# Mixture layers computed by expert: rows sorted through DRAM instead of every token through every expert

## The reference

```python
x = x + 0.5 * _L0_ffn_ref(_layernorm(x, axis=-1), L0_ffn_router_w, ...)
x = x + _L0_attn_ref(_layernorm(x, axis=-1), L0_attn_Wq, ...)
x = x + 0.5 * _L0_ffn_ref(_layernorm(x, axis=-1), L0_ffn_router_w, ...)
```

```python
h_norm = layer_norm(h, rn_g, rn_b)
g = jax.nn.softmax(jnp.einsum('bsd,ed->bse', h_norm, router_w), axis=-1)
top2_w, top2_idx = jax.lax.top_k(g, 2)
top2_w = top2_w / (jnp.sum(top2_w, axis=-1, keepdims=True) + EPS_GATE)
hid = jnp.einsum('bsd,edh->bseh', h, w1)
hid = jax.nn.relu(layer_norm(hid, ln_g, ln_b))
expert_out = jnp.einsum('bseh,ehd->bsed', hid, w2)
...
out = jnp.sum(top2_out * top2_w[..., None], axis=-2)
return layer_norm(out, on_g, on_b)
```

## Time and profile before

| | us |
|---|---|
| median of 3 runs (1240.02 to 1240.84) | 1240.5 |
| span of the profiled execution | 1236.4 |
| PE / DVE / POOL / ACT busy in it | 1140.2 / 948.3 / 672.0 / 512.8 |
| one block of a mixture layer (8 a layer) | 52.2 |
| one block of attention (8) | 35 |

### The profile page before, as it was taken

The page is one execution under the profiler, slowest core; times in us unless marked ns, Lnnn a source line. Parts: engine busy times, 40 slices in busy tenths (PEclk is TensorE's granted clock), DMA queues, the critical chain, the costliest instruction groups (busy, mean ns, idle before and its releaser), DMA issues.

```text
span 1236.4 us, 25066 instructions
## 1 busy us (share of the span) xinstructions
PE 1140.2 (92%) x8694; PEld 731.9 (59%) x8694; DVE 948.3 (77%) x2150; ACT 512.8 (41%) x878; POOL 672.0 (54%) x1039
## 2 busy tenths in 40 slices
PE   4669799999999999889999999889999999999996
PEld 4335456656566566656666666556566665666664
DVE  5678787887978878657777777578879787797875
ACT  4353324233342424456665666442333424334131
POOL 2365546454565544498778777543555654546360
PEclk9789989999999999999999999899999999999998
DMA  9002000000000000000000000000000000000000
GB/s 286 4 1 69 1 1 2 1 2 1 0 0 0 1 2 1 19 18 15 11 13 18 17 18 18 1 2 2 17 1 18 1 19 18 0 17 1 19 18 17
DMA packets 29037, 20.69 MB, mean 17 GB/s; under 512 B 7812, under 2 KB 27784, under 8 KB 28808
## 3 DMA queue, kind: packets, MB, share of 16 engines
q1 hardware_dynamic: 24112, 18.36, 5.4%
q10 hardware_dynamic: 4824, 1.07, 0.5%
HBM read 11.03 MB, written 4.19 MB: 12 GB/s over the span
## 4 chain that ended last, share of the span: by engine, by line
PE 48%; DVE 19%; issue 16%; POOL 10%; ACT 4%; DMA 2%; DVEq 1%; ACTq 0%; POOLq 0%
PE bank L1547 7%; PE bank L1549 6%; PE bank L1548 6%; DVE area L674 5%; DVE area L682 4%; PE bank L1532 4%; PE bank L1534 4%; PE bank L1533 4%; DVE area L655 4%; PE bank L1506 4%; POOL area L487 3%; PE bank L1555 2%; PE bank L1557 2%; PE bank L1556 2%; DMA betas<-in_L_ffn_ln_b_dram 2%
## 5 line engine op out<-in xcount | busy, mean ns | idle before, releaser
L1256 ACT ACTIVATE area<-area 128x512 f16<-128x512 f32 x256 | 160.9, 630 | 387.9 <-DVE area L674 386.1
L1547 PE MATMUL bank<-w2h,area 128*128 128x256 f16 x1024 | 281.3, 275 | 12.9 <-DVE area L693 7.2
L1548 PE MATMUL bank<-w2l,area 128*128 128x256 f16 x1024 | 280.5, 274 | 0.0
L1549 PE MATMUL bank<-w2h,area 128*128 128x256 f16 x1024 | 280.5, 274 | 0.0
L674 DVE SCALAR_TENSOR_TENSOR area<-area,betas,bank 128x512 f32<-128x512 f32 x256 | 189.9, 743 | 46.0 <-PE bank L1534 37.6
L682 DVE SCALAR_TENSOR_TENSOR area<-area 128x512 f16<-128x512 f32 x256 | 188.7, 737 | 20.3 <-ACT area L1256 17.1
L1532 PE MATMUL bank<-hTh,w1h 128*128 128x512 f16 x512 | 195.5, 382 | 6.7 <-DVE area L674 6.7
L1533 PE MATMUL bank<-hTl,w1h 128*128 128x512 f16 x512 | 195.1, 381 | 0.0
L1534 PE MATMUL bank<-hTh,w1l 128*128 128x512 f16 x512 | 194.9, 381 | 0.0
L696 DVE SCALAR_TENSOR_TENSOR area<-bank,coef,area 128x256 f32<-128x256 f32 x192 | 92.1, 482 | 79.3 <-PE bank L1549 78.1
L487 POOL TENSOR_TENSOR area<-area 128x512 f16<-128x512 f32 x96 | 119.9, 1274 | 45.1 <-ACT area L1300 44.9
(11 more groups left out here) (233 smaller groups left out, 2109.6 us busy)
## 6 DMA issues: line engine op xcount, KB each, us to landing
X<-in_L_attn_x_dram SPq DMA_DIRECT2D x8, 512.0 KB, 7.1
area<-area SPq DMA_DIRECT2D x128, 32.0 KB, 2.0
out_dram<-X SPq DMA_DIRECT2D x7, 512.0 KB, 2.9
area<-in_L_ffn_w_dram SPq DMA_DIRECT2D x4, 512.0 KB, 9.9
X<-in_L_ffn_w_dram SPq DMA_DIRECT2D x2, 1024.0 KB, 15.7
area<-in_L_ffn_ln_g_dram ACTq DMA_DIRECT2D x1, 1024.0 KB, 6.1
out_dram<-X SPq DMA_DIRECT2D x4, 128.0 KB, 1.7
area<-in_L_attn_Wq_dram SPq DMA_DIRECT2D x1, 256.0 KB, 9.2
```

The lines of the kernel that those rows point to most:

```text
L1256: act.activation(Rh[:, e % 2, m, :], V[:, a % NV], ACT.Relu).then_inc(s_Rh, 1)
L1547: pe.matmul(dst, Rh[:, e % 2, k, rows], w2h[:, e, k, :], start=(k == 0), stop=False)
L1548: pe.matmul(dst, Rh[:, e % 2, k, rows], w2l[:, e, k, :], start=False, stop=False)
L1549: last = pe.matmul(dst, Rl[:, e % 2, k, rows], w2h[:, e, k, :], start=False, stop=(k == HC - 1))
```

## The change

The loops are written out, and a mixture layer becomes two groups of 16 tiles (GT = 16). For a group, the tokens' normed rows (high and low half, 1 KB a row) are made first, with the router's logits and the two best experts of each token. From counts over all 16 tiles (prefix, 17 small matmuls) DVE works out each row's place in a list that is sorted by expert, each expert's part rounded up to whole tiles of 128 rows: 35 slot tiles (NJ = 2 x 16 + 3). POOL scatters the rows to this list in DRAM (scatter, 32 indirect DMAs of 128 rows, one for each tile and choice). SP loads slot tiles back four ahead (load_slots). PE reads the slot tile's expert number from a table into a register (expert) and takes the expert's weights by this register: transposes, Gram, layer 1 (24 matmuls of 128 columns), layer 2 of the slot before (12 of 256). ACT scales the result (scale_out), SP stores it to DRAM (store_slots), and after the group's 35 slots POOL gathers two rows for each token (gather, two indirect DMAs a tile); ACT and DVE weigh, add and norm them and add to X (first_weighted, token_sum, token_out; add_offset on POOL adds the norm's offset to X ahead). Both lists are cleared first (4.6 MB each, by a transfer of SP), since ends are read too.

Group 1's rows, router and scatter stand inside group 0's slots, group 0's gathers inside group 1's slots from slot 38 on (C_AT). Group 0's rows and scatter stand ahead of slot 0, group 1's gathers behind slot 69. Attention starts when the last tile is added (c_x at NT), mixture 2's rows follow attention's last update. ln_b is loaded as one contiguous row. The cores of the diff:

```diff
+            def load_slots(S):
+                G, J = group(S)
+                if J == 0:
+                    sp.wait_ge(sc_h[G % 2], 16 * 2 * GT * (G // 2 + 1))
+                if S < R_HS:
+                    sp.wait_ge(zeroed[0], 16)
+                wait(sp, b_T, S - R_HS + 1)
+                wait(sp, b_h2, S - R_HS + 1)
+                sp.dma_start(hs[:, S % R_HS].rearrange("p c d -> p (c d)"),
+                             slots_in[G % 2][J * P:(J + 1) * P, :]).then_inc(l_hs[S % R_HS], 16)
+            def store_slots(S):
+                G, J = group(S)
+                sp.wait_ge(b_Y, S + 1)
+                if J == 0 and G >= 2:
+                    sp.wait_ge(c_acc, GT * (G - 1))
+                sp.dma_start(slots_out[G % 2][J * P:(J + 1) * P, :], ysb[:, S % R_Y]).then_inc(st_y[S % R_Y], 16)
+            def mixture(f):
+                S0, S1 = f * SF, (f + 1) * SF
+                for S in range(S0, S0 + 4):
+                    load_slots(S)
+                for S in range(S0, S1 + 2):
+                    if S - 2 >= S0:
+                        store_slots(S - 2)
+                    if S + 4 < S1:
+                        load_slots(S + 4)
 
...
+            def scatter(G):
+                pool.wait_ge(r_pos, G + 1)
+                pool.wait_ge(r_hl, GT * (G + 1))
+                if G < 2:
+                    pool.wait_ge(zeroed[G], 16)
+                else:
+                    pool.wait_ge(b_h2, NJ * (G - 1))
+                for t in range(GT):
+                    for k in range(2):
+                        pool.indirect_dma_start(slots_in[G % 2],
+                                                bass.IndirectOffsetOnAxis(pos[:, G % 2, k, t:t + 1], 0),
+                                                hrow[:, t].rearrange("p c d -> p (c d)"), None
+                                                ).then_inc(sc_h[G % 2], 16)
...
+            def slot_std(S):
+                pool.wait_ge(b_ve, S + 1)
+                wait(pool, b_Y, S - 3)
+                k = S % 4
+                pool.tensor_tensor(stds[:, k], vare[:, k:k + 1].to_broadcast([P, 2]), expo[:, :],
+                                   ALU.pow).then_inc(b_sd, 1)
...
+            def gather(i):
+                G, t = i // GT, i % GT
+                if t == 0:
+                    for r in range(R_Y):
+                        pool.wait_ge(st_y[r], 16 * uses(NJ * (G + 1), r, R_Y))
+                wait(pool, c_acc, i - R_C + 1)
+                for k, d in enumerate((yA, yB)):
+                    pool.indirect_dma_start(d[:, i % R_C], None, slots_out[G % 2],
+                                            bass.IndirectOffsetOnAxis(pos[:, G % 2, k, t:t + 1], 0)
+                                            ).then_inc(g_y[i % R_C], 16)
...
+            def mixture(f):
+                G = 2 * f
+                for k in range(GQ):
+                    quad_rstd(GQ * G + k)
+                    quad_again(GQ * G + k)
+                if f == 0:
+                    for e in range(E):
+                        w1_low(e)
+                scatter(G)
+                if f == 0:
+                    pool.wait_ge(p_mx, 2)
+                    pool.partition_all_reduce(mxa2[:, :], mx2[:, :], P, RMAX).then_inc(p_mxa, 1)
+                    for e in range(E):
+                        w2_low(e)
+                for t in range(GT):
+                    add_offset(GT * G + t)
+                S0 = f * SF
+                slot_std(S0)
+                slot_std(S0 + 1)
+                for s in range(SF):
+                    t = s + 2 - A_AT
+                    if 0 <= t < GT and t % TB == 0:
+                        quad_rstd(GQ * (G + 1) + t // TB)
+                    if s + 2 < SF:
+                        slot_std(S0 + s + 2)
+                    t = s + 1 - A_AT
...
+                    if s == CHAIN_AT + 1:
+                        scatter(G + 1)
+                    t = s - C_AT - 2
+                    if 0 <= t < GT:
+                        token_rstd(GT * G + t)
+                    t = s - C_AT
+                    if 0 <= t < GT:
+                        gather(GT * G + t)
+                for t in range(GT + 1):
+                    if t < GT:
+                        gather(GT * (G + 1) + t)
+                    if t >= 1:
+                        token_rstd(GT * (G + 1) + t - 1)
...
+            def expert(S):
+                G, J = group(S)
+                if J == 0:
+                    pe.wait_ge(r_tab, G + 1)
+                return pe.value_load(etab[0:1, G % 2, J:J + 1], min_val=0, max_val=E - 1)
...
+            def layer1(S, e):
+                pe.wait_ge(b_sdr, S + 1)
+                wait(pe, b_Rl, S - 1)
+                if S == 0:
+                    pe.wait_ge(p_w1l, E)
+                a = hT[:, S % R_HT]
+                for m in range(HC):
+                    o = bank[S % 2][:, m * P:(m + 1) * P]
+                    cols = slice(m * P, (m + 1) * P)
+                    for c in range(KC):
+                        pe.matmul(o, w1h[:, bass.ds(e, 1), c, cols], a[:, c], start=(c == 0), stop=False)
+                        pe.matmul(o, w1h[:, bass.ds(e, 1), c, cols], a[:, KC + c], start=False, stop=False)
+                        last = pe.matmul(o, w1l[:, bass.ds(e, 1), c, cols], a[:, c], start=False, stop=(c == KC - 1))
...
+                for S in range(S0, S1):
+                    s = S - S0
+                    if S + 3 < S1:
+                        slots_T(S + 3)
+                    t = s - A_AT
+                    if 1 <= t <= GT:
+                        rows_T(GT * (G + 1) + t - 1)
+                    if S + 2 < S1:
+                        e[S + 2] = expert(S + 2)
+                        gram(S + 2, e[S + 2])
+                    layer1(S, e[S])
+                    if 1 <= t <= GT:
+                        router(GT * (G + 1) + t - 1)
+                    if S + 1 < S1:
+                        std_T(S + 1)
+                    if s >= 1:
+                        layer2(S - 1, e[S - 1])
+                    if s == CHAIN_AT:
+                        prefix(G + 1)
+                layer2(S1 - 1, e[S1 - 1])
...
-            def layer1(n, par, e, m):
-                a = e * HC + m
-                wait(pe, s_V, NA * n + (a - HC + 1))
-                cols = slice(m * P, (m + 1) * P)
-                o = bank[m][:, :]
-                for c in range(KC):
-                    pe.matmul(o, w1h[:, e, c, cols], hTh[:, par, c, :], start=(c == 0), stop=False)
-                    pe.matmul(o, w1h[:, e, c, cols], hTl[:, par, c, :], start=False, stop=False)
-                    last = pe.matmul(o, w1l[:, e, c, cols], hTh[:, par, c, :], start=False, stop=(c == KC - 1))
-                last.then_inc(s_A, 1)
```

1897 lines of the change are left out of this document (879 added, 1018 removed).

## The result

The changed kernel takes 1480.3 us (four runs, 1476.8 to 1484.6) against 1240.7 of the kernel before. The ratio is 1.194, its 95% interval 1.191 to 1.196. It is slower by 240 us, and 110 us slower than forecast.

A forecast was written before the change was run, and what follows sets the result against it. The prediction took PE's matmul work to bound both mixture layers before, and SP's store-load DMA loop the new slots; leads, slots, scatter holes, tails, attention and end summed to 1370 us, slower than 1240.5, with a range of 1220 to 1560.

The forecast's parts named there:

- the seven terms: Parts of the span: mixture 1 lead 163 us, slots 588, second-group scatters 72, tails 122, attention 326, mixture 2 lead 96, end 3.
- What the change removes: PE's matmul work in mixture layers: 70 slot tiles at 3.4 us, 238 us a layer against 418; about 350 us back in both.
- The slot's period: Time from one slot tile to the next: 4.2 us, bounds 3.4 and 5.5; 140 slots make 588 us.
- the store-load loop: SP's queue: store of slot S-2 stands ahead of load of slot S+4; 4.0 to 4.2 us, taken as the slot's bound.
- Rival 2: PE's sequencer bounds the slots at 5.5 us, through register operations between short matmuls; total 1552 us; chance 0.18.
- The register load: PE reading a slot's expert number from SBUF: in no row, put between 0.03 and 2.0 us.
- The scatter and the second scatter's hole: 32 indirect DMAs on POOL, 42 us; the second group's delays slot 24's std, a PE hole of 36 us, twice: 72.
- c: Time of one indirect DMA in POOL's queue: 1.3 us, the middle of 0.595 to issue and 2.0 to land.
- The lead of mixture 1: Start to first slot: weights to 50 us, rows, choice, scatter, all-reduce, offsets, first Gram chain; 163 us against 74 before.
- The tails: After each mixture layer's last slot, gathers and token sums for 16 tiles, 3.5 us a tile: 61 us, twice, 122.
- Attention's start: Now exposed after all tiles: all-reduce with library loads, memset, norms, rows, queries and keys, SP's issues; 44 us.
- four loops: Candidates for a slot's bound: PE's array 3.4 us, its sequencer 2.85 to 3.85, DMA 4.0 to 4.2, DVE 2.6 to 4.6.

The follow-up runs named there:

- e1: Changed kernel with every slot taking expert 0's weights from fixed addresses, no register loaded or computed on PE: 1378.5 us.
- e3: Changed kernel with layer 1 alone taking expert 0's weights from fixed addresses: 1413.4 us.
- e4: Changed kernel with layer 2 alone taking expert 0's weights from fixed addresses: 1462.0 us.
- e10: Changed kernel with each slot's expert register loaded twice, the second value used: 1569.7 us.
- e2: Changed kernel with the expert register loaded once per group, so addresses made from it are also kept in registers: 1375.8 us.
- e5: Changed kernel with the second group's scatter issued three DMAs after each std from slot 21 to 31, not in one piece: 1417.4 us.
- e11: Changed kernel scattering rows of 512 bytes, the high halves alone, with the same number of DMAs and rows: 1482.8 us.
- e7: Changed kernel with pieces of POOL's queue moved: first groups' offsets into slots, two all-reduces ahead of the first scatter, attention's memset into slots: 1445.5 us.

## Why the prediction was right, and where not

The sign and the range held, and five of the seven terms are off by less than 9 us. The mechanism of the largest term did not hold. By the steps:

- *What the change removes.* The array's price of a slot was right: 3.4 forecast, 3.62 measured where nothing else holds PE (e1). The 0.2 are the two small transposes of the std with the gaps around them. DVE, said to be under 80% before, was at 41.86 of 52.20 us, a shade over.
- *The slot's period.* This step failed. The forecast took the store-load loop, 4.2 us, and it was not the longest: that was the sequencer, which was put at 2.85 us and a load between 0.03 and 2.0, and the period it sets is 4.7. The loop itself was priced too high for most slots: its two issues are 0.32 and 0.38 us and not 0.60 each, it closed in 3.42 us in e1 without a wait and took 3.94 where a load's issue was 1.28, and all its waits in e1 are 8 us. On the sequencer two sizes were wrong; the counts were near (28 register operations beside the load and five waits a slot in the trace, 30 and seven forecast). A register operation costs about 0.048 us in the sum (e3, and e4 in the first layer; 0.025 by e4's second), not 0.032 for an addition by its own row; with the load at 0.64 (e10; the durations of its three operations are 0.47) that is 28 x 0.048 + 0.64 = 1.98. The remaining 2.7 are 46 matmuls and five waits; with 0.05 for a wait, 0.05 for a matmul, not the 0.025 of rows 5, which were matmuls of 16 columns with fixed addresses. This last number is what is left of a sum and was not measured by itself; it is close to the array's own 0.055, so that the runs do not tell how much of it is the sequencer's. Rival 2 named the mechanism and had its price too high (5.5). The Trainium skill ("TensorE: Matmul & The Clock Gate", section "Wait — 56ns, not 53.3ns?") gives about 62 ns for a matmul on the sequencer when hardware decode is off, and the forecast set it aside for fixed addresses; e2's matmuls with held registers, at 0.055, stay under it.
- *The register load.* The Trainium skill ("Runtime: NRT & Kernel Launch", "The ~15µs preamble/postamble breakdown") has about 1.3 us for the TENSOR_LOAD ahead of a kernel, which loads registers from HBM; from SBUF, the trace has 0.302 for one, and e10 has 0.64 with what belongs to it.
- *The scatter and the second scatter's hole.* c was taken at 1.3, the middle between 0.6 and 2.0, with no row of a transfer issued by POOL; it is 1.27. That was luck, and four scatters and the tails rest on it. The hole was put at 36 each and is 38.5, and e5 shows that it was the scatter in POOL's queue: in pieces, both holes are gone.
- *The lead of mixture 1* came 19 us later. Its chain of waits:

```profile
36.12 8.40 issue
...
73.71 1.06 ACT w1h L1174
...
109.08 1.31 POOL slots_in L443
...
149.99 5.58 issue
```

The step that failed is "ACT is free of weights at about 50 us". In the changed kernel POOL pauses 8.40 us behind the first all-reduce and then makes norm factors for four quads, 1 us each time, ahead of the weight products on DVE; ACT's last weight copy ends at 74.8. The rest of the term went as worked out: rows and choice to 109.1, the scatter to 150.0, the all-reduce and w2 to 171.2, offsets 11.25 (forecast 14).
- *The tails.* Forecast 61 each, measured 62.5 and 64.6. Their chain, over two tiles:

```profile
1427.32 1.00 POOL area L484
...
1428.63 2.74 DMA area<-slots_out,pos
...
1434.29 0.99 POOL area L484
```

1427.32 to 1434.29 is 6.97 us for two tiles, 3.5 a tile, as forecast: a gather issued, 2.74 us to land, ACT, DVE, a std on POOL, and the next gather behind it. The old tail, put at 8, is 8.7 us to the last update of X, and the span ends 10.7 us after the last matmul.
- *Attention's start.* Forecast 44 with 282 for the blocks; together 8 less. The chain has the terms that were named; of its pieces, the longest:

```profile
631.38 7.34 issue
```

an all-reduce (623.60), the memset (623.98, 6.87 us), and this pause of 7.34 behind them. The half clock behind the tail, some 2.6 us, was in no term.

The forecast's sum was right to 8%. Most of its terms were priced from rows of the same operation; the transfer's price was a lucky middle. The term that was wrong was the maximum of four loops, and one of the four was priced from rows of another kind of instruction. That the result still lies in the range says little for the loop that was chosen: the bounds given for the period were 3.4 and 5.5 us, and the range was wide enough for both.

## What to carry to other kernels

Work that is saved on a full engine is worth what it frees only if nothing new becomes longer. Here sparse routing cut what PE has to do for a layer's experts from 418 to about 250 us (70 x 3.62), and the order it needs (all rows placed before the first slot, all slots stored before the last gather) exposed 411 us in which PE has little or nothing to do. Price these ends first.

When weights are chosen by a register, count the register operations for each matmul, and keep addresses in registers while the choice stays the same: here addressing is free, making the address is not, and matmuls of 128 columns leave no room for it (0.24 us for three instead of 0.164). When one bound is lifted, read the next one stretch by stretch: here it was ACT's rows in one, DVE's token sums in another, and the array in the third. A hole in PE may stand far from the instructions that cause it.

## What the runs showed of the hardware

- The work of PE's sequencer shows far from where it stands: taking 8 additions out of layer 2 took 0.40 us off a slot of the first layer and closed the hole at the register load (e4); in the second layer it took off 0.20.
- Loading one register from SBUF takes 0.302 us by its row; a second load with its two operations made a slot 0.64 to 0.70 us longer (e10).
- A matmul that takes its weights by a register costs no more than one with a fixed address (1375.8 against 1378.5 us, and 3.62 us for most clean slots in both, e2 and e1).
- An indirect transfer of 128 rows holds POOL for 0.96 us and 0.30 more until the next, with 512 bytes a row as with 1 KB (e11).
- POOL pauses around an all-reduce without waiting for anything that the profile shows: 5.58 us ahead of one (at 149.99), 8.40 and 7.34 behind (at 36.12 and 631.38). The pause behind falls on the next sum or product, even if 32 indirect transfers stand between (e7, 6.71 us), and each pause starts at two MODIFY_POOL_CONFIG in POOL's queue (153.1 in e7).
- A load of 128 KB takes SP 0.38 us to issue in most slots and up to 2.13 in some (e1).
